# Delta stage in 64x64 diagonal halves, key pieces ahead of the turns, and a shorter opening block

## The chip, the cores and the metric

The kernel runs on one NeuronCore of a Trainium2 chip. TensorE (PE) multiplies, VectorE (DVE), ScalarE (ACT) and GpSimd (POOL) work on tiles in SBUF and PSUM, and SyncE (SP) issues most DMAs. The metric is the device time of one execution in microseconds (us); lower is better.

## The reference, cut to what matters

The model is a stack of six layers on x, 2 x 256 tokens of 256 channels: cross-attention over 2 x 4096 context tokens (8 heads), a delta-rule layer, a mixture of experts, a biased cross-attention (16 heads), a quantised attention and a recurrent cell. The change is in the first layer's start and in the delta-rule layer, whose core is this, with 4 heads of 64, chunks of 32 tokens and 8 chunks per batch:

```python
strict_lower = (idx[:, None] > idx[None, :]).astype(q.dtype)
A = -(kb @ jnp.swapaxes(k, -1, -2)) * strict_lower
for i in range(1, chunk):
    A = A.at[..., i, :i].add(jnp.einsum('...j,...jc->...c', A[..., i, :i], A[..., :i, :i]))
T = A + jnp.eye(chunk, dtype=A.dtype)
u = T @ v
w = T @ kb
def step(S, xs):
    qi, ki, ui, wi, g = xs
    attn = qi @ jnp.swapaxes(ki, -1, -2) * tril_inc
    u_t = ui - wi @ S
    o_i = qi @ S + attn @ u_t
    S_new = g[..., None, None] * S + jnp.einsum('bhck,bhcv->bhkv', ki, u_t)
    return (S_new, o_i)
```

T is the inverse of a unit lower triangular matrix of 32 x 32, one for every batch, head and chunk. Everything is float32.

## The kernel before

The six layers are six stages, each a block of five instruction streams (one per engine) that meet at the block's end. Everything is laid out by hand: each stream waits on semaphores that the others count up, and the order within a stream is the order of the code.

*The opening block* (`start`, L69 to L94) stands before the first stage. SyncE issues the first weights (L170), the first of four context chunks (L179; the chunks end at pieces 1, 3, 6 and 8 of eight), x (L78), the other three chunks (L79), and four raw weight matrices of the fifth stage (L80 to L82). VectorE and GpSimd fill three constants. No engine enters the first stage's block before all of this is issued; landings are waited for where data is used.

*The first stage* (`cross_attention`, not biased): PE makes the first pair's key pieces 0 and 1 (`first_keys`, L563, matmuls of L382), transposes the normalised x (`norm_tensor`, L148, L153), adds the output bias by a product, makes the queries (L421) and the key pieces 2 to 7, and then sweeps over pairs of heads. VectorE normalises x once it has landed (L120 to L138) and rounds the raw weights after the eighth piece (`round_weights`, L97). SyncE's stream loads each next pair's weights when PE has used the last (`load`, L323).

*The delta stage* (`delta_rule`, L898). Tokens lie in T = 4 tiles of 128 rows; a tile holds four chunks, and with 4 heads there are M = 16 matrices of 128x128 for each of the tiles AT, X, XT, PR and AQ (L940 to L944), each block-diagonal with four 32x32 blocks. The steps, in order:

1. Loads (L1031 to L1042), then the next attention's weights and context; projections, short convolution, rotation and normalisation of q, k, v. PE makes the next attention stage's key pieces on the side (`next_keys`, L1048; matmuls of L1059), which ScalarE copies out (`next_keys_out`, L1274, L1276): pieces 0 to 5 before the turns, 6 and 7 inside the Gram products at t == 1 (L1110). Between them, `keep_streaming` (L157, L160) runs bf16 matmuls whose result nobody reads.
2. Turns: K, KB and Q are transposed on PE (L1097 to L1106, rows of L1103) and copied by ScalarE (L1293, L1295).
3. Gram products (L1109 to L1130): per tile t three kinds (K with KB, KB with K, K with Q) of four heads each, 128x128 out, contraction 64. VectorE masks them into AT, XT, X and AQ (L1500, L1501, L1503, L1510); the identity is added to X and XT by GpSimd for three tiles (L1388), by VectorE for the last (L1508). At t == 3 PE also transposes the mixer's result (L1119).
4. Inversion (L1131 to L1163, L1511 to L1528): four levels that double the size of the inverted blocks from 2 to 32. Per level and tile, `product(t)` makes AT times X (L1141), VectorE masks it into PR (L1524), `join(t)` makes the corrections of X and XT (L1152, L1155; the last level XT alone), and VectorE adds them (`take`, L1516, L1518). PE works on tile t + 1's product before tile t's join.
5. u = T v (L1166, banks 2 and 3, copied by L1308 and L1540) and w = T kb (L1172, banks 4 and 5, copied negated by L1312 and L1543).
6. The scan over 8 chunks of both batches: `wq_step` (L1181), `ku_step` (L1192, banks 6 and 7), `attend` (L1202), and after it the output projection.

Each 128x128 matrix is used whole by PE though only its diagonal blocks are not zero; each 64x64 diagonal half holds two chunks. PE's array can be addressed in parts: a product whose operands lie in partitions 0 to 63 or 64 to 127, and whose output lies in one of these halves, uses the corresponding quarter (the kernel does this in `attend`). In the rows, a float32 matmul shows as two MATMUL records (passes), and `64*64` ahead of a shape means 64 rows and 64 columns of the array.

## Time and profile before

| | us |
|---|---|
| median of 3 runs (1933.25 to 1935.68) | 1935.21 |
| the profiled execution | 1935.54 |
| its span, first to last instruction | 1933.7 |
| mean granted TensorE clock | 0.977 of 2.4 GHz |
| PE busy | 1852.7 (96%) |
| VectorE busy | 1560.6 (81%) |
| GpSimd busy | 932.9 (48%) |
| ScalarE busy | 861.8 (45%) |

A time of one run is the whole execution; the span is what the trace covers, 1.8 us less. PE counts the matmul records and PEld the weight loads beside them. A row of a timeline has its start, its length, the engine, the line, the operation with out<-in, its shapes and how many instructions it merges; in brackets stands the engine's idle time before it and who ended it. A matmul's end is modelled, so a merged row's length is the starts' distance plus one tail. The first stage covers about 0 to 539 us, the delta stage 539 to 685.6.

### The profile page before, as it was taken

To read this page: it belongs to the slowest core of one execution; us is meant where nothing else is said; L and a number is where in the kernel's file an instruction comes from. 1 tells how busy PE (TensorE), PEld (TensorE's weight loads), DVE (VectorE), ACT (ScalarE), POOL (GpSimd) and SP (SyncE) were. 2 spreads that over 40 slices of the span, in tenths; PEclk is the share of its full clock that TensorE was granted. 3 is DMA by queue.
4 is the path that set the end of the run, shared out by engine and by line. 5 is a ranking of instruction groups with operands and counts; after the bars stand their busy time and mean duration, and the time that the engine had idled before them with its cause. 6 is when DMAs were issued, how large, how long until landed. Compare 5 with 4: busy or idle time off the path is not lost. (4 is left out here: it accounts for less than half of the span.)

```text
span 1933.7 us, 44526 instructions
## 1 busy us (share of the span) xinstructions
PE 1852.7 (96%) x17446; PEld 1269.7 (66%) x17446; DVE 1560.6 (81%) x2167; ACT 861.8 (45%) x1205; POOL 932.9 (48%) x444
## 2 busy tenths in 40 slices
PE   7999999999879989999999999999999999999788
PEld 4667666666647869866666666667666666666545
DVE  4666766676877746699999999999999999999884
ACT  3666666666632235433434344444443343434401
POOL 0347655665652034116655575547655665557300
PEclk9999999999989889999999999999999999999889
DMA  3000110000030043000000000120000000000000
GB/s 139 10 15 0 49 66 14 0 14 9 7 143 1 2 150 98 28 9 2 14 14 14 7 6 14 31 84 0 14 14 14 0 14 14 14 0 10 14 37 11
DMA packets 27773, 52.80 MB, mean 27 GB/s; under 512 B 4259, under 2 KB 15284, under 8 KB 27188
## 3 DMA queue, kind: packets, MB, share of 16 engines
q1 hardware_dynamic: 27232, 51.57, 8.2%
q8 instruction: 57, 0.93, 0.2%
q10 hardware_dynamic: 468, 0.16, 0.0%
q14 instruction: 16, 0.13, 0.0%
HBM read 51.20 MB, written 0.52 MB: 27 GB/s over the span
## 5 line engine op out<-in xcount | busy, mean ns | idle before, releaser
L358 POOL TENSOR_TENSOR biased_sums<-biased_sums,biased_scores 128x1024 f32<-128x1024 f32 x216 | 513.0, 2375 | 137.9 <-ACT biased_scores L663 118.5
L729 DVE TENSOR_TENSOR biased_scores<-ps,bias 128x1024 f32<-128x1024 f32 x256 | 310.9, 1214 | 35.2 <-PE ps L446 33.9
L743 DVE TENSOR_TENSOR ps<-ps,biased_scores 128x512 f32<-128x512 f32 x480 | 331.6, 691 | 4.1
L750 DVE TENSOR_TENSOR biased_scores<-biased_scores,ps 128x1024 f32<-128x1024 f32 x256 | 304.8, 1210 | 3.4 <-PE ps L504 2.7
L663 ACT ACTIVATE biased_scores<-biased_scores 128x1024 f32<-128x1024 f32 x256 | 263.0, 1052 | 97.2 <-DVE biased_scores L750 95.1
L358 POOL TENSOR_TENSOR plain_sums<-plain_sums,plain_scores 128x1024 f32<-128x1024 f32 x104 | 246.6, 2372 | 60.5 <-ACT plain_scores L663 50.1
L743 DVE TENSOR_TENSOR ps<-ps,plain_scores 128x512 f32<-128x512 f32 x240 | 167.3, 697 | 118.2 <-ACT plain_scores L646 113.3
L446 PE MATMUL ps<-biased_queries,keys_again 64*128 64x256 f32 x2048 | 257.3, 390 | 3.6 <-DVE biased_scores L729 2.8
L458 PE MATMUL ps<-biased_scores,biased_values 128*64 128x256 f32 x2048 | 245.2, 381 | 3.6 <-ACT biased_scores L663 3.2
L393 PE MATMUL ps<-weights_again,context_again 128*64 128x128 f32 x4096 | 247.9, 274 | 0.0
L393 PEld LDWEIGHTS ps<-weights_again,context_again 128*64 128x64 f32 x4096 | 228.5, 137 | 28.8 <-issue 17.9
L382 PE MATMUL ps<-context_again,weights_again 128*64 128x512 f32 x960 | 228.1, 601 | 0.0
L446 PEld LDWEIGHTS ps<-biased_queries,keys_again 64*128 64x128 f32 x2048 | 187.7, 187 | 53.7 <-issue 24.8
L458 PEld LDWEIGHTS ps<-biased_scores,biased_values 128*64 128x64 f32 x2048 | 145.5, 138 | 105.2 <-issue 47.4
L358 POOL TENSOR_TENSOR biased_sums<-biased_scores 128x1024 f32<-128x1024 f32 x16 | 38.1, 2381 | 324.1 <-ACT biased_scores L663 324.1
L624 ACT ACTIVATE keys_again<-ps 128x512 f32<-128x512 f32 x120 | 71.3, 594 | 259.1 <-PE ps L382 259.1
L635 ACT ACTIVATE biased_values<-ps 128x512 f32<-128x512 f32 x128 | 76.5, 598 | 239.2 <-PE ps L393 239.2
L750 DVE TENSOR_TENSOR plain_scores<-plain_scores,ps 128x1024 f32<-128x1024 f32 x128 | 152.0, 1210 | 3.5 <-PE ps L504 3.1
L663 ACT ACTIVATE plain_scores<-plain_scores 128x1024 f32<-128x1024 f32 x128 | 130.6, 1051 | 38.4 <-DVE plain_scores L750 36.5
L646 ACT ACTIVATE plain_scores<-ps 128x1024 f32<-128x1024 f32 x128 | 124.1, 1021 | 25.0 <-PE ps L446 25.0
L382 PE MATMUL ps<-context,weights 128*64 128x512 f32 x512 | 123.2, 611 | 11.9 <-PEq L72 11.9
L382 PEld LDWEIGHTS ps<-context_again,weights_again 128*64 128x64 f32 x960 | 61.0, 136 | 110.7 <-issue 110.7
(410 smaller groups left out, 2279.3 us busy)
## 6 DMA issues: line engine op xcount, KB each, us to landing
moe_w<-in_moe_w SPq DMA_DIRECT2D x32, 256.0 KB, 2.7
weights_again<-in_wqkv SPq DMA_DIRECT2D x45, 128.0 KB, 2.2
context<-in_ctx_t SPq DMA_DIRECT2D x4, 1024.0 KB, 6.7
context_again<-in_ctx_t SPq DMA_DIRECT2D x4, 1024.0 KB, 7.4
bias<-in_fside SPq DMA_DIRECT2D x1, 4096.0 KB, 15.7
biased_w_out<-in_w_out SPq DMA_DIRECT2D x16, 256.0 KB, 2.6
context<-in_ctx_t SPq DMA_DIRECT2D x2, 1536.0 KB, 9.2
context_again<-in_ctx_t SPq DMA_DIRECT2D x2, 1536.0 KB, 9.8
```

The source lines that it names most:

```text
L358: pool.tensor_tensor(both(SUM[:, :, :, :]), both((E[:, 0] if kp == 1 else SUM)[:, :, :, :]), both(E[:, kp, :, :, :]), ALU.add).then_inc(su ...
L382: last = pe.matmul(c.ps[half, bank, :], W[:, 1, i, half], CT[:, i, g * KG:(g + 1) * KG], start=(i == 0), stop=(i == DC - 1))
L393: last = pe.matmul(c.ps[half, bank, n * P:(n + 1) * P], CT[:, i, at + half.start:at + half.stop], W[:, 2, i, :], start=(i == 0), stop=(i = ...
L446: last = pe.matmul(out, KT[half, at:at + P], QS[half, :].rearrange("p (t j) -> p t j", t=2), start=True, stop=True)
L458: last = pe.matmul(c.ps[n * HD:(n + 1) * HD, OUT, h * S:(h + 1) * S], VS[:, 2 * kp + n, h * HD:(h + 1) * HD], E[:, kp, 2 * h:2 * h + 2, n, :],
L624: act.activation(KT[:, g * KG:(g + 1) * KG], c.ps[:, bank, :], ACT.Copy).then_inc(piece_kept, 1)
L635: act.activation(VS[:, 4 * g:4 * g + 4, :].rearrange("p a n -> p (a n)"), c.ps[:, piece_bank(m, which), :], ACT.Copy).then_inc(piece_kept, 1)
L646: act.activation(both(E[:, kp, :, :, :]), scores_bank(kp), ACT.Copy).then_inc(scores_kept, 1)
L663: act.activation(at, at, ACT.Exp).then_inc(exp_done, 1)
L729: dve.tensor_tensor(E[:, kp, :, :, :].rearrange("p (h t) n j -> p h t (n j)", h=2), scores_bank(kp).rearrange("p (h t n) -> p h t n", h=2, ...
L743: ins = dve.tensor_tensor(to, highest, E[:, kp, :, n, :], ALU.max)
L750: dve.tensor_tensor(at, at, c.ps[:, LOWER, :].rearrange("p (a j) -> p a j", a=HQ).unsqueeze(2) .to_broadcast([P, HQ, 2, P]), ALU.add).then ...
```

## The change

1. `start` issues only the weights, the first context chunk and x. The other three chunks and the raw weights (new function `load_raw_weights`) are issued by SyncE at the head of the first stage's block.
2. PE's stream of the first stage begins with six matmuls of 128x128 on the constant ones, into bank 7.
3. The five kinds of matrices are kept as their two diagonal halves, one above the other in the partitions: [128, 16, 64] instead of [128, 16, 128]. The masks likewise, with the identity as a ninth one; their DMA is 9 x 64 instead of 8 x 128 floats per partition.
4. The work is cut in two units of two tiles (8 matrices) instead of four tiles (4 matrices). A PE product is two matmuls of 64x64, one for each half. VectorE's and GpSimd's operations keep 512 elements per partition and are half as many; GpSimd adds the identity for the first unit, VectorE for the second.
5. In the levels PE runs both products, then both joins. Each unit has its own bank.
6. Key pieces 6 and 7 are made ahead of the turns, with five fillers left out; KB's turn waits for the last of their copies. ScalarE copies pieces 4 and 5 before its second root and 6 and 7 right behind it.
7. w uses banks 4 to 7; both first `ku_step`s come behind the waits for all copies of u and w.

```diff
             load_weights(c, sync, a["wqkv0"], 0)
             load_context(c, sync, a["ctx_t"], 0, range(1))
             sync.dma_start(c.X[:, :, :], a["x"].rearrange("b (u p) d -> p (b u) d", p=P)).then_inc(c.x_in, 16)
-            load_context(c, sync, a["ctx_t"], 0, range(1, CONTEXT_CHUNKS))
-            for i, n in enumerate("qkvo"):
-                sync.dma_start(c.WRAW[:, i, :, :], a[f"L1_attn_w{n}"].rearrange("(j p) n -> p j n", p=P)
-                               ).then_inc(c.w_raw_in, 16)
...
+def load_raw_weights(c, queue, raw):
+
+    for i, w in enumerate(raw):
+        queue.dma_start(c.WRAW[:, i, :, :], w.rearrange("(j p) n -> p j n", p=P)).then_inc(c.w_raw_in, 16)
...
+                if not biased:
+                    load_context(c, sync, ctx_t, 0, range(1, CONTEXT_CHUNKS))
+                    load_raw_weights(c, sync, raw)
                 load(START - 1)
...
                 else:
+                    for n in range(6):
+                        pe.matmul(c.ps[:, LOWER, 0:P], c.ones[:, :], c.ones[:, :], start=True, stop=True)
                     first_keys(0)
                     first_keys(1)
...
-    masks += [pairs(m).astype(np.float32) for m in (2, 4, 8, 16)]
-    return np.ascontiguousarray(np.stack(masks, 1))
+    masks += [pairs(m).astype(np.float32) for m in (2, 4, 8, 16)] + [np.eye(P, dtype=np.float32)]
+    halves = np.stack(masks, 1).reshape(2, P // 2, len(masks), 2, P // 2)
+    return np.ascontiguousarray(np.concatenate([halves[x, :, :, x, :] for x in range(2)]))
...
-        MASK = sb("masks", [P, 8, P])
+        MASK = sb("masks", [P, 9, HD])
...
-        AT = sb("a_t", [P, M, P])
...
+        AT = sb("a_t", [P, M, HD])
...
-            return (0, 6, 7, 0, 6, 7, 0, 1)[g]
+            return (0, 6, 7)[g % 3]
...
-            return WQ[:, u, :, :, 3 * CH * r:(3 * r + 1) * CH].rearrange("p t x c -> p (t x) c")
+            return WQ[:, u, :, :, 3 * CH * r:(3 * r + 1) * CH]
...
-            return c.ps[:, 4 + u, :].rearrange("p (y c) -> p y c", c=2 * CH)[:, :, r * CH:(r + 1) * CH]
+            return c.ps[:, 4 + 2 * u:6 + 2 * u, 0:T * HD].rearrange("p x (t c) -> p t x c", c=HD)[:, :, :, r * CH:(r + 1) * CH]
...
-        def gram(kind, t, h):
-            at = h // 2 * P
-            return c.ps[:, 2 + 2 * kind + h % 2, at:at + P]
...
+        def gram(kind, t, h, x):
+            at = (t % 2 * 2 + h // 2) * HD
+            return c.ps[HALVES[x], 2 + 2 * kind + h % 2, at:at + HD]
...
-                next_keys(5)
-                pe.wait_ge(norm_sums, 1)
-                keep_streaming(c, pe, 5, 2)
+                for g in range(5, KEY_PIECES):
+                    next_keys(g)
                 for bank, rows, ready, count in ((4, K, k_ready, 1), (6, KB, k_ready, 2), (0, Q, q_ready, 1)):
                     if bank == 6:
-                        pe.wait_ge(piece_kept, KEYS_BEFORE + 6)
+                        pe.wait_ge(piece_kept, KEYS_BEFORE + KEY_PIECES)
...
-                for t in range(T):
-                    if t == 1:
-                        for g in range(6, KEY_PIECES):
-                            next_keys(g)
-                    if t == T - 1:
-                        pe.wait_ge(piece_kept, KEYS_BEFORE + KEY_PIECES)
...
+                for u in range(UNITS):
                     for kind, (left, right) in enumerate([(1, 2), (2, 1), (1, 0)]):
-                        if t >= 1:
-                            pe.wait_ge(grams_kept, 3 * (t - 1) + kind + 1)
+                        if u >= 1:
+                            pe.wait_ge(grams_kept, 3 * (u - 1) + kind + 1)
                         elif kind == 2:
                             pe.wait_ge(turned_kept, 3)
-                        for h in range(H):
-                            last = pe.matmul(gram(kind, t, h), turned_rows(left, h, t), turned_rows(right, h, t),
+                        for t in (2 * u, 2 * u + 1):
+                            for pair in range(H // 2):
+                                for x in range(2):
+                                    for h in (2 * pair, 2 * pair + 1):
+                                        last = pe.matmul(gram(kind, t, h, x), turned_rows(left, h, t, x),
+                                                         turned_rows(right, h, t, x), start=True, stop=True)
+                        last.then_inc(grams, 1)
...
+                def blocks(bank, u, left, right):
+                    for m in range(u * UM, (u + 1) * UM):
+                        at = m % UM * HD
+                        for half in HALVES:
+                            last = pe.matmul(c.ps[half, bank, at:at + HD], left[half, m, :], right[half, m, :],
                                              start=True, stop=True)
-                        last.then_inc(grams, 1)
+                    return last
+
...
-                    def product(t):
-
-                        pe.wait_ge(x_kept, 2 * (T * lev + t + 1))
...
-                            pe.wait_ge(grams_kept, 3 * (T - 1) + 1)
-                        for h in range(H):
-                            last = pe.matmul(c.ps[:, 2 + t % 2, h * P:(h + 1) * P], AT[:, t * H + h, :],
-                                             X[:, t * H + h, :], start=True, stop=True)
-                        last.then_inc(p_done, 1)
-
-                    def join(t):
-                        pe.wait_ge(p_kept, T * lev + t + 1)
...
-                            pe.wait_ge(grams_kept, 3 * T)
-                        for h in range(H if lev < 3 else 0):
-                            pe.matmul(c.ps[:, 4 + t % 2, h * P:(h + 1) * P], XT[:, t * H + h, :],
-                                      PR[:, t * H + h, :], start=True, stop=True)
-                        for h in range(H):
-                            last = pe.matmul(c.ps[:, 6 + t % 2, h * P:(h + 1) * P], PR[:, t * H + h, :],
-                                             XT[:, t * H + h, :], start=True, stop=True)
-                        last.then_inc(x_done, 1)
-
-                    product(0)
-                    for t in range(T):
-                        if t + 1 < T:
-                            product(t + 1)
-                        join(t)
...
-                for m in range(M):
-                    last = pe.matmul(bank2(2)[:, m * HD:(m + 1) * HD], XT[:, m, :], U[:, m, :],
-                                     start=True, stop=True)
-                    if m % (M // B) == M // B - 1:
-                        last.then_inc(uw_done, 1)
+                    def product(u):
+
+                        pe.wait_ge(x_kept, 2 * (UNITS * lev + u + 1))
+                        if lev == 0:
+                            pe.wait_ge(grams_kept, 3 * (UNITS - 1) + 1)
+                        blocks(2 + u, u, AT, X).then_inc(p_done, 1)
+
+                    def join(u):
+                        pe.wait_ge(p_kept, UNITS * lev + u + 1)
+                        if lev == 0:
+                            pe.wait_ge(grams_kept, 3 * UNITS)
+                        if lev < 3:
+                            blocks(4 + u, u, XT, PR)
+                        blocks(6 + u, u, PR, XT).then_inc(x_done, 1)
+
+                    for u in range(UNITS):
+                        product(u)
+                    for u in range(UNITS):
+                        join(u)
+                pe.wait_ge(x_kept, 2 * UNITS * 5)
+                for u in range(UNITS):
+                    blocks(2 + u, u, XT, U).then_inc(uw_done, 1)
                 for t in range(T):
                     for h in range(H):
-                        last = pe.matmul(c.ps[lane(h), 4 + h // 2, t * P:(t + 1) * P], KB[:, t * H + h, :],
-                                         XT[:, t * H + h, :], start=True, stop=True)
+                        for x, half in enumerate(HALVES):
+                            last = pe.matmul(c.ps[lane(h), 4 + h // 2 * 2 + x, t * HD:(t + 1) * HD],
+                                             KB[half, t * H + h, :], XT[half, t * H + h, :], start=True, stop=True)
...
-                pe.wait_ge(uw_kept, 1)
-                ku_step(0, 0)
-                pe.wait_ge(uw_kept_dve, 1)
-                ku_step(0, 1)
                 pe.wait_ge(uw_kept, 3)
                 pe.wait_ge(uw_kept_dve, 3)
+                ku_step(0, 0)
+                ku_step(0, 1)
...
-                for s in range(2):
-                    if s == 0:
-                        act.wait_ge(act_step, M)
-                    else:
-                        act.wait_ge(norm_sums, 2)
-                    act.activation(NS[:, s, :], NQ[:, s, :], ACT.Sqrt, bias=NEPS[:, 0:1]).then_inc(norm_roots, 1)
+                act.wait_ge(act_step, M)
+                act.activation(NS[:, 0, :], NQ[:, 0, :], ACT.Sqrt, bias=NEPS[:, 0:1]).then_inc(norm_roots, 1)
                 for g in range(4, 6):
+                    next_keys_out(g)
+                act.wait_ge(norm_sums, 2)
+                act.activation(NS[:, 1, :], NQ[:, 1, :], ACT.Sqrt, bias=NEPS[:, 0:1]).then_inc(norm_roots, 1)
+                for g in range(6, KEY_PIECES):
                     next_keys_out(g)
...
-                eye = c.ident[:, :].unsqueeze(1).to_broadcast([P, H, P])
-                for t in range(T - 1):
-                    mats = slice(t * H, (t + 1) * H)
-                    pool.wait_ge(grams_kept, 3 * t + 2)
-                    for inverse in (X, XT):
-                        pool.tensor_tensor(inverse[:, mats, :], inverse[:, mats, :], eye, ALU.add).then_inc(x_kept, 1)
+                eye = MASK[:, 8, :].unsqueeze(1).to_broadcast([P, UM, HD])
+                pool.wait_ge(grams_kept, 2)
+                for inverse in (X, XT):
+                    pool.tensor_tensor(inverse[:, unit(0), :], inverse[:, unit(0), :], eye, ALU.add).then_inc(x_kept, 1)
...
-                for t in range(T):
-                    mats = slice(t * H, (t + 1) * H)
-                    src = [grams_of(kind, t) for kind in range(3)]
-                    dve.wait_ge(grams, 3 * t + 1)
...
+                for u in range(UNITS):
+                    mats = unit(u)
+                    src = [grams_of(kind) for kind in range(3)]
+                    dve.wait_ge(grams, 3 * u + 1)
...
                 for lev in range(4):
-                    def take(t):
-                        mats = slice(t * H, (t + 1) * H)
-                        dve.wait_ge(x_done, T * lev + t + 1)
+                    for u in range(UNITS):
+                        dve.wait_ge(p_done, UNITS * lev + u + 1)
+                        dve.tensor_tensor(PR[:, unit(u), :], heads(c.ps[:, 2 + u, :]), mask(4 + lev),
+                                          ALU.mult).then_inc(p_kept, 1)
+                    for u in range(UNITS):
+                        dve.wait_ge(x_done, UNITS * lev + u + 1)
                         if lev < 3:
-                            dve.tensor_tensor(X[:, mats, :], X[:, mats, :], heads(c.ps[:, 4 + t % 2, :], P),
+                            dve.tensor_tensor(X[:, unit(u), :], X[:, unit(u), :], heads(c.ps[:, 4 + u, :]),
                                               ALU.add).then_inc(x_kept, 1)
-                        dve.tensor_tensor(XT[:, mats, :], XT[:, mats, :], heads(c.ps[:, 6 + t % 2, :], P),
+                        dve.tensor_tensor(XT[:, unit(u), :], XT[:, unit(u), :], heads(c.ps[:, 6 + u, :]),
                                           ALU.add).then_inc(x_kept, 1 if lev < 3 else 2)
...
-                    for t in range(T):
-                        mats = slice(t * H, (t + 1) * H)
-                        dve.wait_ge(p_done, T * lev + t + 1)
-                        dve.tensor_tensor(PR[:, mats, :], heads(c.ps[:, 2 + t % 2, :], P), mask(4 + lev),
-                                          ALU.mult).then_inc(p_kept, 1)
-                        if t >= 1:
-                            take(t - 1)
-                    take(T - 1)
```

## Rows read from the trace of the kernel before

**Rows 1.** the page: busy us, share of the span and instructions of each engine

```profile
PE 1852.7 (96%) x17446; PEld 1269.7 (66%) x17446; DVE 1560.6 (81%) x2167; ACT 861.8 (45%) x1205; POOL 932.9 (48%) x444
```

**Rows 2.** timeline of the first 22 us: start, us, engine, line, op, operands

```profile
2.19 2.06 SPq L179 DMA_DIRECT2D context<-in_ctx_t  x3
...
6.60 4.66 SPq L81 DMA_DIRECT2D w_raw<-in_L_attn_wo  x1
...
11.85 6.25 PE L382 MATMUL ps<-context,weights 128*64 128x512 f32 x16 [11.85 <-PEq L72]
...
14.10 1.38 DVE L138 TENSOR_SCALAR XN<-X,moments,inverse 128x256 f32<-128x256 f32 x4
...
18.04 1.10 PE L153 MATMUL ps<-ident,XN 128*128 128x128 f32 x8
```

**Rows 3.** DMA issues of the first 4 us, in windows: KB, us to landing

```profile
context<-in_ctx_t SPq DMA_DIRECT2D x1, 512.0 KB, 4.5
...
X<-in_x SPq DMA_DIRECT2D x1, 512.0 KB, 6.0
...
context<-in_ctx_t SPq DMA_DIRECT2D x1, 1024.0 KB, 8.0
...
context<-in_ctx_t SPq DMA_DIRECT2D x1, 1536.0 KB, 11.3
```

**Rows 4.** waits from 547 to 553 us: total, times, longest

```profile
ACT delta_mix L1254 <- DMA delta_mixer_norm<-in_L_attn_mixer_norm_w: 9.1, 1, 9.1
```

**Rows 5.** timeline of the delta stage up to its first Gram product

```profile
583.57 1.24 PE L160 MATMUL ps<-w_int 128*128 128x512 bf16 x5
...
584.88 0.31 ACT L1288 ACTIVATE delta_norm_roots<-delta_norms,delta_norm_eps 128x16 f32<-128x16 f32 x1 [1.36 <-DVE delta_norms L1476]
...
586.78 1.67 PE L1103 MATMUL ps<-ident,delta_k 128*128 128x128 f32 x8 [1.97 <-DVE delta_k L1472]
...
588.78 1.22 DVE L1472 TENSOR_TENSOR delta_q<-delta_q,delta_norm_inverses 128x1024 f32<-128x1024 f32 x1
...
592.13 1.16 PE L1128 MATMUL ps<-delta_channels_first 64*128 64x128 f32 x16
```

**Rows 6.** timeline of the delta stage, within its Gram products

```profile
593.67 3.70 PE L1059 MATMUL ps<-context_again,weights_again 128*128 128x512 f32 x8
...
594.93 1.27 POOL L1388 TENSOR_TENSOR delta_inv<-delta_inv,ident 128x512 f32<-128x512 f32 x1 [11.54 <-DVE delta_inv L1503]
```

**Rows 7.** timeline of the inversion's levels, PE and one pair of VectorE's

```profile
604.47 2.02 PE L1141 MATMUL ps<-delta_inv,delta_a_t 128*128 128x128 f32 x16 [0.59 <-DVE delta_inv_t L1501]
...
618.08 1.28 DVE L1524 TENSOR_TENSOR delta_product<-ps,delta_masks 128x512 f32<-128x512 f32 x2
...
618.81 1.16 PE L1152 MATMUL ps<-delta_product,delta_inv_t 128*128 128x128 f32 x8 [0.19 <-DVE delta_product L1524]
...
629.99 1.16 PE L1152 MATMUL ps<-delta_product,delta_inv_t 128*128 128x128 f32 x8 [0.19 <-DVE delta_product L1524]
...
647.80 3.79 PE L1166 MATMUL ps<-delta_u,delta_inv_t 128*128 128x64 f32 x32 [0.85 <-DVE delta_inv_t L1518]
```

**Rows 8.** small products: timeline and the two lines' durations (min/median/max)

```profile
653.41 0.68 PE L1192 MATMUL ps<-delta_u,delta_k 32*64 32x64 f32 x16
...
654.63 0.88 PE L1181 MATMUL ps<-delta_state,delta_w_and_q_t 64*64 64x64 f32 x16 [0.54 <-DVE delta_state L1563]
...
L1192 PE MATMUL ps<-delta_u,delta_k x112: 217/309/363, 653.4 to 671.6; 32*64 32x64 f32 x112
...
673.10 1.97 PE L1202 MATMUL ps<-delta_u,delta_attn_t 64*64 64x64 f32 x32
...
L1202 PE MATMUL ps<-delta_u,delta_attn_t x64: 311/311/365, 664.1 to 674.8; 64*64 64x64 f32 x64
```

**Rows 9.** windows in the scan: PE, PEld, DVE, ACT, POOL busy (count), PEclk, DMA share, GB/s

```profile
656.00:660.00 4.00, 3.14 (x56) 2.46 (x56) 3.34 (x11) 0.94 (x3) 0.00 (x0) 0.85 0.00 0
...
660.00:664.00 4.00, 3.86 (x56) 3.12 (x52) 3.10 (x11) 1.32 (x4) 0.00 (x0) 0.50 0.00 0
```

73 lines of the change are left out of this document (33 added, 40 removed).

## The prediction, made before the changed kernel ran

> **What bounds the kernel now.** I read the page's busy table first, then timelines of the two places that the change touches, and the DMA issues. TensorE (PE) is busy 96% of the span, no other engine over 81% [rows 1]. The chain that ended last lies wholly in the last stage, so it says nothing of the two places; what they are worth has to be read there. The stages run one behind the other, and the two attention stages are PE's: a microsecond taken off the start, or off the delta stage, comes off the end.
>
> *Start.* PE's first matmul comes at 11.85 us, released by the end of the opening block (L72), not by data [rows 2]. That block ends when SyncE has issued all its DMAs, the last of which alone holds its queue from 6.60 to 11.26 us [rows 2]. The data was there: the first context chunk landed 4.5 us and x 6.0 us after issues that were all made before 2.19 [rows 2, 3], so at 5.7 and 7.7 (issued at 1.2 and 1.7).
>
> *Delta stage.* Three pieces: up to the first Gram product (592.13), from there to the first product of the inversion (604.47), and the inversion to 647.80, where T times v begins [rows 5, 7]. In the inversion PE never waits for long: a level takes 629.99 - 618.81 = 11.18 us for 96 passes of 128x128 (an f32 matmul is two passes), 0.116 us each [rows 7]. VectorE, with 12 operations a level of which two take 1.28 us, 0.6 apart [rows 7], fits beneath. So the size of PE's work sets the pace there, and the quarters of the array off the diagonal multiply zeros.
>
> **The change part by part.** The profiled execution took 1935.54 us (span 1933.7), 0.3 above the median of the runs, 1935.21. The sum is made against 1935.5.
>
> *1. Opening block.* SyncE is done after x, at about 2.15 us, and with the 0.4 us between 11.26 and the first instructions after it PE is free at 2.6. The six added matmuls are 12 passes; at the slow pace at which PE started before (16 passes of 512 columns in 6.25 us, 0.39 each where two halves share the array [rows 2]) they end by 5.4, before the first chunk lands, so they cost nothing; should they run into it, under 1 us. The first key piece goes 5.7 to 8.2-9.2. The second needs the second chunk: issued at 2.2, landed at 10.2 [rows 2, 3]; it is now issued 0.4 later, behind x that is under way until 7.7, so I leave its landing. Then 1.7 us (fast) or 3.4 (if PE is slow again after waiting) for the piece, and the transposes of the norm begin at 11.9 to 13.6 in place of 18.04. XN was there 3.8 us after VectorE could begin (11.7 to 15.5 [rows 2]), so now at 7.7 + 3.8 = 11.5, in time. The third chunk landed near 14.2 [rows 2, 3], the fourth, 1024 KB behind it, by that rate near 16.8; the pieces that need them, the fourth and the seventh, lie one and four pieces of 1.7 us behind the queries, which come 2 us after the transposes, so from 16 and 21 on: hidden. SyncE's later weight loads stand behind the moved issues, which are through by 12 as before, and wait for the queries anyway. ScalarE's small bias load is issued 9 us earlier with them and not needed before 13. VectorE reads the raw weights only after the eighth piece. **Saved 5.3 (4.4 to 6.1).**
>
> *2. Masks.* 295 KB replace 524. By the context chunks (1536 KB in about 4 us, [rows 3]) that is at most 0.55 us; the stage's ScalarE and then VectorE wait for the last of these loads [rows 4]. But small transfers lie between, so 0 to 0.5. **Saved 0.2.**
>
> *3. Key pieces ahead of the turns.* PE runs five fillers from 583.57 and then waits 1.97 us for K at 586.78 [rows 5]. Pieces 6 and 7, 8 passes in 3.70 us with the tail of the last [rows 6], so 1.7 each, take 583.57 to 587.0 in their place: 0.2 past K. ScalarE's copies of pieces 4 and 5, 0.6 each, now stand before its second root; that root waited 1.36 us for its input at 584.88 [rows 5], and both fit into that wait. KB's turns wait for the last piece's copy, 0.8 behind the piece, so 587.8, while VectorE still makes KB (it is at Q from 588.78 on). Q's turns hang on Q, 588.78 + 1.22 = 590.0 [rows 5]; with 0.9 for them and 0.7 for the three fillers the Gram products start at 591.6, 0.5 earlier. The pieces' real return is that 3.70 us leave the middle of the Gram products [rows 6].
>
> *4. Gram products.* Six groups of 32 passes of 64x64. Price of such a pass: at the full clock, 16 passes of 32x64 took 0.68 with a last one of 0.217, so (0.68 - 0.22)/15 = 0.031; at the low clock 32 passes of exactly the new shape took 1.97 with 0.311, so 0.0535 [rows 8]. At 0.031 a group is 1.0 us. VectorE needs 4 x 0.6 for the first unit and 6 x 0.6 for the second, GpSimd 2 x 1.27 [rows 6] beside it, done by 597.2; none holds PE up. 591.6 + 6.0 + 1.0 for the eight fractal transposes: first product at 598.6. **Saved 604.5 - 598.6 = 5.9 (4 to 6.5).**
>
> *5. Inversion.* A level is product, product (1.0 each), join, join (2.0 each). VectorE does 6 operations in place of 12. What is late next: the second product needs both sums of its unit, taken after the last join: the tail of 0.2, 1.28 for the two, 0.07 to hand over, 1.55 after the joins end [rows 7, 8], while the first product covers 1.0. A level is 1.55 + 1.0 + 2.0 + 2.0 = 6.5; the first, with no such wait, 6.0. The last: 1.55 + 3 x 1.0, then 0.95 until the last sum is there (0.85 of wait before [rows 7]), 5.5. 6.0 + 6.5 + 6.5 + 5.5 = 24.5 against 43.3. **Saved 18.8 (17.5 to 20).**
>
> *6. T times v and kb, first step.* 64 passes of 0.031 for 32 in 3.7 us [rows 7]; w is 64 passes in 2.0. The first state update now waits for all copies of w, because w fills the banks that it writes; before, both ran side by side in the 1.2 us from 653.41 to 654.63 [rows 8], so it costs 0 to 1.2, and I take 0.45, since the copies were most of it. From 647.80 to 654.63 is 6.8 before, 5.9 after. **Saved 0.9.** Less 1.6 (0 to 3): the scan ran its first steps at the full clock [rows 9], and it and w will now follow 20 us of small products and a wait of 0.95.
>
> Sum: 5.3 + 0.2 + 5.9 + 18.8 + 0.9 - 1.6 = 29.5. **1935.5 - 29.5 = 1906.0 us.** The attend products keep their shape: nothing.
>
> **The rivals.** *A. The low clock reaches into the inversion.* The granted clock was 1.00 (2.4 GHz) for all of the 128x128 levels. It fell to 0.50 (1.2 GHz) within 656 to 660, during the scan's products of 32x64 and 64x64 with waits between, and stayed there from 660 to 664 although PE counts as busy 3.86 of 4 us with the same shapes [rows 9]. The new levels are made of such passes alone, with a wait in each. Against it: their streams of 5 us are denser than the scan's. If it falls in the second level: 6.0 + 8.4 + 10.3 (six units of 32 at 0.0535: 1.7 + 1.7 + 3.4 + 3.4) + 7.9 = 32.6, saved 10.7; part 6 loses 1.9, the scan 0.7. 5.3 + 0.2 + 5.9 + 10.7 - 1.9 - 0.7 = 19.5: **1916.0**. A fall in the third level gives 1911.
>
> *B. The halves don't share the array: slower than before.* The two halves of a product write the same PSUM bank. One after the other, 64 columns cost half of 0.116, 0.058, at the full clock and 0.116 at the low one. With the low clock too, the three levels are 6 x 32 x 0.116 = 22 us each and the last 15, 81 against 43.3; part 6 loses 8, the Gram products another 8 or so: 11.4 - 8 - 38 - 8 = -43, **1978**. It decides from about 0.066 us a pass on (832 passes from the first product to w, to be done in the 50 us of before plus the 11 saved elsewhere, less 6 of waits). Against it, 32 passes that are such diagonal halves of one bank took 1.97 us, 0.0535 each, at the low clock, where one after the other they would take 3.7 [rows 8]. The Trainium skill says the opposite of what this row shows (TensorEngine Tiling (Array Packing), Restrictions and Gotchas): row tiles write to different PSUM banks and can't access one bank at the same time. By that rule this case would be the outcome; the trace disagrees with it, for halves that write different partitions.
>
> *C. The start gives nothing* because the first piece is held by something other than L72's block, or the second chunk lands later now that it is issued later: 1906 + 5.3 = **1911**. *D. The moved pieces hold the turns* by a copy's wait: at most a piece, **1908**.
>
> **How the numbers follow.** The forecast, 1906.0, has 0.52; its own bounds (4.4 to 6.1, 0 to 0.5, 4 to 6.5, 17.5 to 20, 0.9 less 0 to 3) put it between 1903 and 1910. A has 0.34 with its partial form, C and D 0.11 together, B 0.03. Leaving out B, late forms of A and the best tenth gives 1902 to 1918. A measurement of this kernel tells 0.2% (3.9 us) from no change: faster 0.96, same 0.01, slower 0.03.
>
> **What would show it.** Right: PE's first filler near 2.7 us and the norm's transposes at 12 to 13.6; no PE gap between 583 and 587 of the old count; the first product 6 us after the first Gram product or 7; groups of 32 passes in 1.0 to 1.2 us; levels 6.5 us apart with one PE wait of 0.5 for VectorE in each; granted clock 1.00 through the levels. Wrong: a clock of 0.50 with groups of 1.9 (A); 32 passes over 2 us at the full clock (B); levels of 6.5 us but VectorE the one waited for in every join.

## The result, and the profile after

The changed kernel takes **1905.68 us** (median of 5 runs, 1905.12 to 1906.91) against 1935.68 (1933.25 to 1938.48) of the kernel before in the same session: ratio 0.9851, 95% interval 0.984 to 0.9862. The profiled execution took 1906.91, its span 1905.1, so 28.6 less than the span before. The forecast was 1906.0.

The opening (timeline; columns as in [rows 2]):

```profile
2.55 1.40 SPq L181 DMA_DIRECT2D context<-in_ctx_t  x3
2.59 2.90 PE L607 MATMUL ps<-ones 128*128 128x128 f32 x12 [2.59 <-PEq L72]
5.60 2.90 PE L387 MATMUL ps<-context,weights 128*64 128x512 f32 x8
6.11 5.36 SPq L167 DMA_DIRECT2D w_raw<-in_L_attn_wo  x1
10.49 3.24 PE L387 MATMUL ps<-context,weights 128*64 128x512 f32 x8 [2.00 <-DMA context<-in_ctx_t]
13.66 1.43 PE L149 MATMUL ps<-ident,XN 128*128 128x128 f32 x8
```

PE starts at 2.59 and not at 11.85 [rows 2], while the transfer that held it (6.11 to 11.47) now holds SyncE alone. The second key piece waits 2.00 us for its context chunk, and then takes 3.24 us where 1.94 is the length at the full clock (start_filled, below). The norm's transposes start 4.38 us earlier.

From the turns to the first state update (timeline of PE):

```profile
583.99 1.04 PE L1114 MATMUL ps<-ident,delta_k 128*128 128x128 f32 x8
585.69 1.06 PE L1114 MATMUL ps<-ident,delta_kb 128*128 128x128 f32 x8 [0.67 <-DVE delta_kb L1485]
...
588.70 1.16 PE L1130 MATMUL ps<-delta_channels_first 64*64 64x64 f32 x64
589.68 0.65 PE L1130 MATMUL ps<-delta_w_and_q_t,delta_channels_first 64*64 64x64 f32 x32
...
594.06 1.15 PE L1145 MATMUL ps<-delta_inv,delta_a_t 64*64 64x64 f32 x32
...
600.43 1.10 PE L1145 MATMUL ps<-delta_inv,delta_a_t 64*64 64x64 f32 x32
601.99 1.15 PE L1145 MATMUL ps<-delta_inv,delta_a_t 64*64 64x64 f32 x32 [0.46 <-DVE delta_inv_t L1518]
602.97 1.10 PE L1145 MATMUL ps<-delta_product,delta_inv_t 64*64 64x64 f32 x32
603.90 1.10 PE L1145 MATMUL ps<-delta_inv_t,delta_product 64*64 64x64 f32 x32
...
606.70 1.10 PE L1145 MATMUL ps<-delta_inv,delta_a_t 64*64 64x64 f32 x32
...
618.48 2.02 PE L1145 MATMUL ps<-delta_u,delta_inv_t 64*64 64x64 f32 x62 [0.86 <-DVE delta_inv_t L1518]
...
623.20 0.68 PE L1196 MATMUL ps<-delta_u,delta_k 32*64 32x64 f32 x16 [1.71 <-DVE delta_w_and_q_t L1534]
624.03 0.98 PE L1185 MATMUL ps<-delta_state,delta_w_and_q_t 64*64 64x64 f32 x16 [0.15 <-DVE delta_state L1554]
```

Read it beside [rows 5 to 8]. K's turns begin with no gap. The first two Gram groups, 64 passes, take 589.68 - 588.70 = 0.98 us: 0.015 each. The blocks of a level start 0.93 apart, 0.029 a pass, and a level is 606.70 - 600.43 = 6.27 us (11.18 before), with one wait of 0.46 for VectorE. The granted clock (windows, columns as in [rows 9]):

```profile
612.00:616.00 4.00, 3.55 (x122) 3.41 (x120) 2.77 (x6) 0.00 (x0) 0.00 (x0) 1.00 0.02 4
...
620.00:624.00 4.00, 2.17 (x100) 1.92 (x96) 3.27 (x7) 0.93 (x3) 0.00 (x0) 1.00 0.00 0
624.00:628.00 4.00, 3.51 (x56) 2.79 (x56) 3.29 (x11) 1.50 (x4) 0.00 (x0) 0.67 0.01 4
628.00:632.00 4.00, 3.76 (x54) 2.96 (x50) 3.18 (x10) 0.75 (x2) 0.00 (x0) 0.50 0.00 0
```

It stays at 1.00 through the levels, T times v and w, and falls only in the scan. Where the 28.6 us come from, by the starts of the same instructions in both profiles:

| stretch | before | after | saved |
|---|---|---|---|
| start to the first queries | 20.45 | 16.41 | 4.04 |
| to the delta stage's norm transposes | 522.64 | 523.85 | -1.21 |
| to the first Gram product | 49.04 | 48.44 | 0.60 |
| to the first product of the inversion | 12.34 | 5.36 | 6.98 |
| inversion, to T times v | 43.33 | 24.42 | 18.91 |
| T times v, w and first state update, to the first product of W and Q | 6.83 | 5.55 | 1.28 |
| scan, to the last output projection | 29.62 | 30.16 | -0.54 |
| all that follows | 1249.45 | 1250.91 | -1.46 |

Nothing in the second and the last row was edited (of the second, only some transfers are issued later). The experiments say how much such rows move by themselves. Of the second row the granted clock (third number from the end) tells more. The window lies near the end of that stretch; first the kernel before, then the changed one:

```profile
494.00:516.00 22.00, 16.86 (x142) 11.10 (x140) 14.66 (x21) 9.39 (x12) 6.99 (x5) 0.84 0.05 13
```
```profile
494.00:516.00 22.00, 16.85 (x122) 9.78 (x117) 15.31 (x20) 10.21 (x11) 5.95 (x4) 0.77 0.05 13
```

Of all thirteen profiles, the two in which the clock of this window was 1.00 (halves_apart, gram_quarters) have 521.2 us in that row, and the six with 0.77, the changed kernel's among them, 523.7 to 524.1. Why the clock falls there in some executions and not in others, no run shows.

### The profile page after: what moved, and what is told of

It reads as the page before. It is cut to its first block and busy times, and to the rows that moved or that the text cites. A ratio compares the mean times of both kernels' runs of the same rounds, so it can differ in the third digit from the quotient of the medians.

```text
span 1905.1 us, 45489 instructions
## 1 busy us (share of the span) xinstructions
PE 1832.0 (96%) x17954; PEld 1250.4 (66%) x17965; DVE 1541.2 (81%) x2137; ACT 861.9 (45%) x1205; POOL 927.4 (49%) x440
## 5 line engine op out<-in xcount | busy, mean ns | idle before, releaser
L451 PE MATMUL ps<-plain_queries,plain_keys 64*128 64x256 f32 x1024 | 127.9, 389 | 0.0
```

What stands on the lines that cost most here:

```text
L451: last = pe.matmul(out, KT[half, at:at + P], QS[half, :].rearrange("p (t j) -> p t j", t=2), start=True, stop=True)
```

## The experiments

Most times of one kernel lie within 2 to 4 us of their median, some farther off (start_only, twelve runs: 1925.76 to 1934.29), so an effect of 2 us is read from the profile's stretches and not from the median. The masks alone (part 2 of the prediction) had no run of their own.

**Does the start's gain last?** The kernel before with the opening part alone (the transfers behind x moved out of the first block, six fillers). Expected:

> The kernel before with the change's opening part alone (fewer transfers in the first block, six fillers); masks and delta stage stay as they were. Theory: the start is worth what the changed kernel's trace shows by the first key stream, 4.04 us (queries at 16.41 in place of 20.45), and nothing gives it back: 1935.5 - 4.0 = 1931.5 us, ratio 0.998. Rival 1, the prediction's own term: 5.3 us, 1930.2. Rival 2: the 1.5 us that the changed kernel lost again between 499 and 514 us belongs to the earlier start and comes back here, so that the delta stage begins only 2.5 us earlier: 1933.0 us.

1929.11 us (median of 12 runs) against 1934.01; ratio 0.9976 (0.9965 to 0.9987): 4.6 us, 2.5 to 6.8, which leaves the theory and rival 1 open and speaks against rival 2. The queries came at 14.54, 5.9 earlier and not 4.04: the start itself scatters, as the next runs show. This profile did lose 1.5 us again up to the delta stage (524.11 for 522.64), as rival 2 had it, and with it the low clock near 500 us; other profiles with the same opening lose nothing there (521.2).

**Was the slow second piece the wait's doing?**

```
                    first_keys(0)
+                   for n in range(5):
+                       pe.matmul(c.ps[:, LOWER, 0:P], c.ones[:, :], c.ones[:, :], start=True, stop=True)
                    first_keys(1)
```

> The changed kernel with five more filler matmuls (10 passes) between the first and the second key piece, where PE waits 2.0 us for the second context chunk. Theory: PE's slow pace in the second piece (3.24 us for 8 passes, 1.7 at the fast pace) comes from that wait; without the wait the piece takes 1.7 us from 10.5 on, the transposes begin at 12.2 in place of 13.66, and the whole time is 1.5 us less: 1904.2. Rival 1: the pace stays slow for a stretch after the start whatever PE does, so the fillers change nothing or run up to 0.6 us into the piece: 1905.7 to 1906.3. Rival 2: XN, ready at 11.7, or the copy of XNT then holds the queries: 1904.7.

1904.27 us (1902.41 to 1905.36), ratio 0.9841 (0.9828 to 0.9854). Timeline of PE, and the window of 11 to 14 us:

```profile
7.77 1.38 PE L610 MATMUL ps<-ones 128*128 128x128 f32 x10
9.79 1.94 PE L387 MATMUL ps<-context,weights 128*64 128x512 f32 x8 [0.64 <-DMA context<-in_ctx_t]
11.66 1.09 PE L149 MATMUL ps<-ident,XN 128*128 128x128 f32 x8
```
```profile
11.00:14.00 3.00, 2.38 (x14) 1.15 (x10) 1.23 (x3) 0.60 (x1) 0.00 (x0) 1.00 1.01 411
```

The same window of the changed kernel:

```profile
11.00:14.00 3.00, 3.00 (x10) 0.78 (x7) 0.72 (x3) 0.23 (x1) 0.00 (x0) 0.50 1.02 421
```

So the slow piece is a granted clock of 0.50 after the wait. But of the ten profiled kernels with this opening and no such fillers, whose starts are the same code, four had the fast piece (1.94) too and six took 3.08 to 3.68; with the fillers it was fast in both profiles that there are, in one of them (rows_spread) after a wait of 1.60 us all the same. Nor does the length of the wait sort the ten: the fast pieces came after 0.67, 1.69, 2.51 and 3.08 us of it, the slow ones after 1.96 to 3.01. So that the wait makes the piece slow is not shown, and the 1.4 us between the medians are within the scatter. The chunk itself came anywhere from 9.70 to 11.37.

**How large is chance?** The changed kernel again:

> The changed kernel once more, unchanged, beside runs of the kernel before on the same chip. Theory: what earlier runs of unchanged stretches showed (queries first at 13.97 to 16.62 us, the first stage 521 to 524 us long, 173 to 177 us from the delta stage's end to the fourth stage's first scores) is chance that no edit causes; so the median is 1904 to 1906 us, and the profile's queries may start anywhere between 14.0 and 16.6. Rival: each build has its own start; then the queries come at 16.4 again.

1906.14 us (1901.6 to 1908.27); ratio 0.9846 (0.9831 to 0.9861). The median is 0.14 above the range expected; the start was the slowest of all, beyond the range that I had given:

```profile
11.37 3.68 PE L387 MATMUL ps<-context,weights 128*64 128x512 f32 x8 [3.01 <-DMA context<-in_ctx_t]
14.97 1.97 PE L149 MATMUL ps<-ident,XN 128*128 128x128 f32 x8
```

Its queries came at 18.26. Over ten profiles with the unchanged new opening they came between 13.97 and 18.26, 15.77 on average: **4.7 us saved, 2.2 to 6.5 in a single run**, against the one profile of the kernel before. At the delta stage's norm transposes these ten are 4.7 us earlier on average too (2.0 to 6.7), so on average nothing is given back on the way. Over all thirteen profiles the second row of the table, from the queries to the delta stage, took 521.2 to 524.1, and its last row, all behind the delta stage, 1248.1 to 1254.8. The -1.21 and -1.46 of the table lie within that. The scan's row took 29.6 in both profiles with the old delta stage; of the ten with the new one and no fillers in the scan, eight have 30.1 to 31.1, and two less than before (29.47 in this run, 28.04 in two_banks). So its -0.54 is usual, but not sure.

**Key pieces ahead of the turns**, undone (pieces 6 and 7 back between the units, fillers and ScalarE's order as before):

> The changed kernel with the seventh and eighth key piece back between the two units of Gram products and the five fillers back ahead of the turns. Theory: the two pieces' 3.4 to 3.7 us come back whole into the Gram part, the turns begin no earlier than before because K isn't there, so the first product of the inversion comes 3.5 us later against the stage's start: 1905.7 + 3.5 = 1909.2 us. Rival: VectorE's and GpSimd's masking of the first unit would have held PE up there anyway, so that less than 1.5 us comes back: 1907 us or less.

1906.57 us (1906.05 to 1913.83), ratio 0.9855 (0.9835 to 0.9875), which can't tell 3.5 from 0. The profile can: to the first Gram product 49.05 us (48.44), from there to the first product 7.77 (5.36), 3.0 together; the six profiles with the changed kernel's code up to there took 53.2 to 53.8 for both, so 3.0 to 3.6. The theory holds, and the rival, under 1.5, falls.

**The halves must alternate.** In blocks():

```
-                   for m in range(u * UM, (u + 1) * UM):
-                       at = m % UM * HD
-                       for half in HALVES:
+                   for half in HALVES:
+                       for m in range(u * UM, (u + 1) * UM):
+                           at = m % UM * HD
```

> The changed kernel with all first halves of a block issued before all second halves, in the inversion and in T times v; the same passes in another order. Theory: two halves run in the array at once only because they alternate. Apart, a pass costs twice the 0.029 us, 0.058, a block of 32 passes 1.86 us in place of 0.93, a level 11.2 us in place of 6.27; 22 blocks of the four levels and 2 of T times v give 24 x 0.93 = 22, less 1.4 of waits that are then covered: 1905.7 + 21 = 1927 us. Rival: the pace is set by the issue of instructions or by the weight loads, and the order makes no difference: 1905.7 us, blocks of 0.93 us.

1917.51 us (1913.97 to 1919.85), ratio 0.9906 (0.9885 to 0.9927): 12 us slower, not 21. Timeline of PE, the first blocks and the first product of two levels:

```profile
594.32 1.50 PE L1145 MATMUL ps<-delta_product,delta_inv_t 64*64 64x64 f32 x26
595.60 0.27 PE L1145 MATMUL ps<-delta_inv_t,delta_product 64*64 64x64 f32 x1
595.65 0.22 PE L1145 MATMUL ps<-delta_product,delta_inv_t 64*64 64x64 f32 x1
...
595.83 1.50 PE L1145 MATMUL ps<-delta_inv_t,delta_product 64*64 64x64 f32 x26
...
597.33 1.50 PE L1145 MATMUL ps<-delta_product,delta_inv_t 64*64 64x64 f32 x26
...
600.35 3.26 PE L1145 MATMUL ps<-delta_inv,delta_a_t 64*64 64x64 f32 x58
...
609.66 3.26 PE L1145 MATMUL ps<-delta_inv,delta_a_t 64*64 64x64 f32 x58
```

A block is 1.51 us and a level 9.31. The inversion took 35.19 us (24.42), and T times v to the first state update 6.80 (4.72); in that last stretch the clock fell as well (0.57 from 628 to 632 us). The distances from start to start (us) show why:

```
halves apart:   0.058 0.059 0.058 0.058 0.059 0.058 | 0.006 0.052 0.054 0.005 0.054 0.004 0.054 | 0.058 0.059 0.058
changed kernel: 0.007 0.051 0.007 0.052 0.006 0.052 0.007 0.051
```

A pass whose neighbours use the same half costs 0.058, as expected; but where the order switches halves, three passes of the next half start beside the last three of this one. It does so between two blocks too, against the order of the program: at 595.60 a pass of delta_inv_t with delta_product starts, and at 595.65 one of the block in front of it. 32 x 0.0585 - 2 x 3 x 0.0585 = 1.52. The pace hangs on the order, and the rival falls; PE makes up for a wrong order over three passes only.

**Two quarters or four?** The Gram passes with the loop over x outermost (gram_apart), and in runs of eight on one quarter (gram_quarters):

> The changed kernel with the Gram products' loop over the halves outermost: consecutive passes still alternate between the two row halves of the array, but no longer between its two column halves. Theory: in the changed kernel four quarters of the array work at once, 0.015 us a pass; with two at once a pass costs 0.029, a group of 32 passes 0.93 us in place of 0.47, so the Gram part is 6 x 0.46 = 2.8 us longer: 1908.5 us. Rival: the column halves bring nothing and the pace of 0.015 has another cause (short waits, modelled ends): no change, 1905.7 us, groups of 0.47.

> The changed kernel with the Gram passes ordered so that eight neighbouring passes use the same quarter of the array. Theory: a pass costs 0.058 us where its neighbours use the same quarter, and some three passes overlap over each of the four changes of quarter in a group, so a group of 32 passes takes 32 x 0.0585 - 4 x 3 x 0.0585 = 1.2 us in place of 0.5, and the first product of the inversion comes 8 to 9.5 us after the first Gram product in place of 5.36. Rival: the order of the passes doesn't matter for Gram products, whose groups had waits for VectorE anyway: below 6.0 us.

1905.09 us (1903.62 to 1906.5) and 1904.17 (two runs): again too close for the times. From the first Gram product to the first product: 5.36 in the changed kernel, 5.89 and **8.24** here. Two groups of 64 passes (timeline of PE; first row of each to the next group's first row), first x outermost, then by quarters:

```profile
586.24 1.39 PE L1130 MATMUL ps<-delta_channels_first 64*64 64x64 f32 x58
587.42 0.27 PE L1130 MATMUL ps<-delta_w_and_q_t,delta_channels_first 64*64 64x64 f32 x2
```
```profile
585.26 2.51 PE L1130 MATMUL ps<-delta_channels_first 64*64 64x64 f32 x61
587.56 0.27 PE L1130 MATMUL ps<-delta_w_and_q_t,delta_channels_first 64*64 64x64 f32 x1
```

1.18 and 2.30 us, against 0.98. The quarters behaved as expected (2 x 1.2 = 2.4). For x outermost both expectations missed, in the same way as above: 32 x 0.029 - 2 switches x 6 passes x 0.029 = 0.58 a group, and 0.59 was measured. So four quarters work at once in the changed kernel, at 0.015 a pass, two at 0.029, one at 0.058.

**Do halves of one PSUM bank hinder each other?** The first product's halves in two banks:

```
-                        blocks(2 + u, u, AT, X).then_inc(p_done, 1)
+                        for m in range(u * UM, (u + 1) * UM):
+                            at = m % UM * HD
+                            for x, half in enumerate(HALVES):
+                                last = pe.matmul(c.ps[half, 2 + (u + x) % 2, at:at + HD], AT[half, m, :],
+                                                 X[half, m, :], start=True, stop=True)
+                        last.then_inc(p_done, 1)
...
```

VectorE's masking of the product becomes one operation for each half.

> The changed kernel with the two halves of AT x X written to two PSUM banks (bank 2 + (unit + half) mod 2), so VectorE masks each half by an operation of its own; the other blocks of a level keep both halves in one bank. Theory: sharing one bank costs nothing, so a block of 32 passes of the first product takes 0.93 us as the joins' blocks do; VectorE has two more operations of 0.6 a unit, which come on top of the waits of a level: levels of 7.5 us in place of 6.27, 1905.7 + 4 to 6. Rival (two row halves cannot write one bank at once, and lose time to it): the product's block of 32 passes falls to some 0.5 us while the joins' stay at 0.93.

1903.29 us (two runs, 1900.62 and 1905.97). Timeline of PE, product (two banks) and join (one bank):

```profile
589.81 1.15 PE L1159 MATMUL ps<-delta_inv,delta_a_t 64*64 64x64 f32 x32
...
593.12 1.15 PE L1145 MATMUL ps<-delta_product,delta_inv_t 64*64 64x64 f32 x32 [0.77 <-DVE delta_product L1517]
```

Both 1.15. One bank costs nothing, and the rival falls. The masking in two operations made the inversion 2.3 us longer (26.73), less than the 4 to 6 expected; it doesn't show in the time, since the profiled run (1900.62) had a low clock that ended earlier in the scan (28.87 us from the first state update to the last projection, 30.99 in the changed kernel) and 6.5 us less in stretches that nothing edited.

**Filling the scan's waits** (four fillers ahead of the first step, behind an added wait for the fractal rows, and two after each step):

> The changed kernel with fillers of 512 columns in the scan's waits (four ahead of the first step, two after each step's products). Theory: the scan's 0.75 us of loss, and the stretch at a granted clock of 0.50 from 625 to 652 us, come from PE's small products; fillers keep the clock at 1.00, and the scan gets 0.7 to 1.5 us shorter: 1904.5 us. Rival: the scan hangs on hand-overs between the engines and the fillers, 0.2 us each, stand in the way of them: 0 to 3 us longer, 1905.7 to 1908.7.

1909.02 us (1907.22 to 1909.58), ratio 0.9866 (0.9851 to 0.9881). Windows:

```profile
618.00:622.00 4.00, 2.97 (x42) 1.87 (x42) 3.14 (x10) 1.18 (x4) 0.00 (x0) 0.91 0.00 0
622.00:626.00 4.00, 3.82 (x44) 2.35 (x42) 2.40 (x8) 0.98 (x3) 0.00 (x0) 0.50 0.01 4
```

Neither: the clock fell all the same, with PE busy 3.8 of 4 us, and the fillers stood in the way at half pace; the scan took 36.90 us for 30.99, twice what the rival allowed (the median is only 3.3 us up, as untouched stretches of this profile are shorter by chance). What lowers the clock there stays open.

**What bounds it now.** First VectorE's sums started as soon as each block is done, and finer waits:

```
...
-                            blocks(4 + u, u, XT, PR)
-                        blocks(6 + u, u, PR, XT).then_inc(x_done, 1)
+                            blocks(4 + u, u, XT, PR).then_inc(x_done, 1)
+                        blocks(6 + u, u, PR, XT).then_inc(x_done, 1 if lev < 3 else 2)
...
```

> The changed kernel with earlier sums: VectorE adds to X as soon as its own block is done, not after both blocks of the join; a product waits for X alone, and each unit of T times v for its own XT. Theory: the wait for VectorE is all that a level has beside its six blocks: 6 x 0.93 = 5.6 us a level in place of 6.27, and the wait of 0.86 ahead of T times v goes: 3 x 0.5 + 0.9 = 2.3 us, 1903.4 us. Rival: VectorE sets the pace (six operations of 0.6 and their hand-overs a level), the waits only move to the joins, and less than 0.7 us comes off: 1905 us or more.

1904.34 us (1901.16 to 1905.91), ratio 0.9834 (0.9821 to 0.9848). The inversion took 21.85 us for 24.42, and the level 5.67 with no wait, as the theory had it. But the first state update followed T times v by 5.65 us and not 4.72:

```profile
611.74 2.02 PE L1145 MATMUL ps<-delta_u,delta_inv_t 64*64 64x64 f32 x61
...
617.40 0.85 PE L1197 MATMUL ps<-delta_u,delta_k 32*64 32x64 f32 x16 [2.64 <-DVE delta_w_and_q_t L1536]
```

VectorE's timeline has the reason. After the last sum it makes the fractal rows, and only then the copies that the scan waits for:

```profile
611.93 0.69 DVE L1520 TENSOR_TENSOR delta_inv_t<-delta_inv_t,ps 128x512 f32<-128x512 f32 x1 [0.25 <-PE ps L1145]
612.54 0.17 DVE L1524 RECIPROCAL delta_frac_scale<-delta_frac_squares 128x4 f32<-128x4 f32 x1
612.74 0.17 DVE L1525 TENSOR_TENSOR delta_frac_scale<-delta_frac_scale,delta_gates 128x4 f32<-128x4 f32 x1
612.94 1.66 DVE L1527 SCALAR_TENSOR_TENSOR delta_frac_rows<-ps,delta_frac_scale,delta_mixer_norm 128x256 f32<-128x256 f32 x4
614.64 1.23 DVE L1531 TENSOR_TENSOR X<-X,delta_frac_rows 128x1024 f32<-128x1024 f32 x1
615.90 0.69 DVE L1533 COPY delta_u<-ps 128x512 f32<-128x512 f32 x1
```

From the start of the last sum to the state update is VectorE's queue, 5.47 us in both kernels, so PE's earlier T times v just waits longer. Hence a version with these sums, the opening's fillers, and the fractal rows one by one in the levels' waits:

```
...
+                        row = 2 * (lev - 1) + u
+                        if lev in (1, 2):
+                            if row > 0:
+                                fractal_add(row - 1)
+                            fractal_row(row)
...
```

> The changed kernel with three edits: the earlier sums, the five fillers between the first two key pieces, and VectorE's 3.3 us of fractal rows (two small operations, four rows of 0.42, the addition to X of 1.23) moved out of the stretch between the last sum and the copies of u and w, a row at a time into the waits of the second and third level. Theory: with early sums the level's bound is PE (5.67 us), and after T times v VectorE's fractal rows are what holds the first state update: 2.64 us of wait in place of 1.71. With them out of the way, from the first product of T times v to the first state update it is 3.8 us in place of 4.72 (5.65 with early sums alone); inversion 21.9 us in place of 24.4: 2.5 + 0.9 = 3.4 us off the delta stage, 1902 us. Rival: the rows, 0.75 us in each of four waits of 0.25 to 0.32, make VectorE late in the levels, and what the end gains the levels lose: from the first product to the first state update 27 us or more in place of 29.1.

**1899.05 us** (1897.99 to 1900.72), ratio 0.9817 (0.9803 to 0.983): faster than both kernels, 6.6 below the changed one.

```profile
612.25 2.08 PE L1147 MATMUL ps<-delta_inv_t,delta_product 64*64 64x64 f32 x64 [0.30 <-DVE delta_product L1523]
...
614.26 2.02 PE L1147 MATMUL ps<-delta_u,delta_inv_t 64*64 64x64 f32 x61
...
618.26 0.68 PE L1199 MATMUL ps<-delta_u,delta_k 32*64 32x64 f32 x16 [0.98 <-DVE delta_w_and_q_t L1550]
```

From the first product to the first state update it is 26.79 us (29.14 in the changed kernel, 27.51 with early sums alone): the inversion lost 0.94 to the rows (22.79), the rest gained 1.65 (4.00). Theory and rival were both partly right. Of the 6.8 us between the two profiled spans, 2.6 lie between the first Gram product and the first state update; 1.7 are an earlier start, by the fillers or by chance, 1.4 the end behind the biased stage, and 1.1 the other stretches, within what they scatter by. So 2.6 us of the gain are shown to be the version's own; with what the fillers may give at the start, 3 to 4 is an estimate. All five runs (1897.99 to 1900.72) lie below all ten of the changed kernel (1901.6 to 1908.27).

## Why the prediction was right, and where it wasn't

Its number is right to 0.3 us, and that is in part luck: the mechanisms were right, but parts 2 to 6 gave 3.0 us more than forecast, the opening 1.3 less, and stretches that nobody edited took back 2.7.

*Bounds.* Right: PE was held at the start by L72's block, and the inversion by the size of PE's products. Once both were lifted, 28.6 us came off the end.

*1, opening, 5.3 (4.4 to 6.1).* The mechanism was right. The profiled run gave 4.04, the profiles' mean is 4.7, and the opening alone measured 4.6. The bounds were too narrow: they held the landing of the second chunk at 10.2 and the pace of one piece open, while both varied, the landing from 9.70 to 11.37. In the profiled run the slow clock also reached into the norm's transposes, 0.34 us more.

*2 and 3, 0.2 and 0.5 to the first Gram product:* 0.60 measured. K's turns did begin with no gap. Undoing part 3 costs 3.0 to 3.6.

*4, first product 5.9 earlier:* with part 2's 0.2, 6.1; measured 7.58. **The term that was mis-sized is the pass of 64x64 in the Gram products, 0.031 us by 16 passes of 32x64 [rows 8].** It is 0.015, and the first product came 0.9 us earlier than the range's best end (6.5) allowed. The step took for granted that a pass shares the array with one other, as in that row; these alternate over both row halves and both column halves. A group is 0.49 us, not 1.0; then VectorE's masks hold PE up (0.48 us before the fourth group), so the part is 5.36 and not 7.0.

*5, inversion, 18.8:* 18.9 measured. The second and third level were 6.27 for the 6.5 worked out, with the second product's wait of 0.46 as foreseen; the pass was 0.029 for 0.031. The first was 6.37 for 6.0: the step gave it no wait, and its second product waited 0.25 for VectorE's identity.

*6, 0.9 less 1.6 for the low clock.* The first measured 1.28. The second is too large: w and T times v ran at the full clock, and the scan lost 0.54, 1.4 at most in ten profiles and nothing in two. The clock did fall sooner, to 0.67 in the window from 1 to 5 us behind the first state update, where [rows 9] have 0.85 from 3 to 7; where it cost anything, it was mostly a third of what I had put down for it.

So parts 2 to 6, forecast at 24.2, gave 27.2 (0.60 + 6.98 + 18.91 + 1.28 - 0.54); the opening gave 1.3 less than forecast and stretches that nothing changed 2.7 less (1.21 + 1.46; of this 1.5 behind the delta stage). In another execution these could have gone the other way.

*Rivals.* A didn't come: 1.00 through all levels. B didn't: the halves shared the array within one bank at 0.029 a pass at the full clock, and it made no difference to give them two banks. The Trainium skill (TensorEngine Tiling (Array Packing), Restrictions and Gotchas) has it that different row tiles can't access one bank at once; for row halves that write different partitions of the bank these runs disagree, and for the same partitions no run shows it. Rival B's price for the unshared pass, 0.058, was right to the third digit, as runs of one half showed; unshared, the levels would have been as long as before. C didn't come: the opening alone gave 4.6. D didn't: K's turns follow the moved pieces without a gap.

## What to carry to other kernels

Block-diagonal work in halves pays twice, through the products that are left out and through the quarters of the array that then work at once, but only if neighbouring passes go to different quarters; count how many quarters a loop's order touches within some three passes before pricing one of them. When a stage gets shorter, look on the other engines' queues for work that had been hidden in it: here 3.3 us of VectorE's rows became what the scan waited for. And put into the range of a small start effect what the same start does from run to run.

## What the runs showed of the hardware

- Passes of 64x64 in f32 at the full clock: 0.058 us on one quarter, 0.029 over two, 0.015 over four, with starts 0.002 to 0.008 apart (after, halves_apart, gram_apart, gram_quarters). PE starts up to three passes of another quarter early, ahead of passes that stand before them in the program, and hides a poor order in short runs (halves_apart: 1.51 us a block and not 1.87). The Trainium skill (TensorE: Matmul & The Clock Gate) says in Part 1 that start to start never drops below about 25 ns, and in Part 3 that matmuls on different tiles start about 4 ns apart; over different quarters these rows agree with the second.
- The same start gave queries between 13.97 and 18.26 us, with a granted clock between 0.50 and 1.00 in the stretch from 11 to 14. That a kernel's cold stretch varies between runs stands in the Trainium skill (TensorE: Matmul & The Clock Gate, Part 1), and the ten profiles agree.
- In the scan the clock stood at 0.50 although PE was busy 3.8 of 4 us with small products, and fillers of 512 columns in its waits didn't lift it (scan_filled, 622 to 630 us).
